# Turning the rows of queries and keys by an F32R product with an F32R identity instead of a transpose

## The reference

```python
q = (x @ wq.T); k = (x @ wk.T); v = (x @ wv.T)      # 16 heads of 8
diff_sq = q_norm_sq + k_norm_sq - 2.0 * qk
denom = maximum((1 - q_norm_sq) * (1 - k_norm_sq), 1e-6)
dist = arccosh(maximum(1 + 2 * diff_sq / denom, 1.0))
out = (softmax(-dist) @ v) @ wo.T
```

## Time and profile before

| | |
|---|---|
| Median of 3 runs | 2456.44 us (2451.4 to 2459.8) |
| Profiled execution, its own time | 2463.32 us |
| Its span | 2461.5 us |
| Mean granted clock of TensorE | 0.917 |
| Busy: PE, DVE, ACT, POOL | 2101.2, 1952.3, 1742.9, 1589.3 us |
| L1363 (turns of rows), MATMUL x1024 | 179.6 us busy |

### The profile page before, as it was taken

One profiled execution on the slowest core, in us unless ns is written; L12 is line 12 of the kernel. 1 busy time (PEld: TensorE's weight loads), 2 busy tenths in 40 slices (PEclk: granted clock), 3 DMA queues, 4 the chain that ended last, 5 costly groups with the idle time before them and its releaser, 6 DMA issues. The chain is left out here.

```text
span 2461.5 us, 50910 instructions
## 1 busy us (share of the span) xinstructions
PE 2101.2 (85%) x15592; PEld 1593.8 (65%) x15592; DVE 1952.3 (79%) x5939; ACT 1742.9 (71%) x3053; POOL 1589.3 (65%) x1609
## 2 busy tenths in 40 slices
PE   4999999999999997999996687778777878778776
PEld 4677777777777776888884455555555555555555
DVE  4677676777777775778776889999999999999982
ACT  2666666666666663444432799999999999999995
POOL 2767676666666740000002889999999898899992
PEclk7999999999999996999997569999999889998987
DMA  5000000000000003453440556666666666566663
GB/s 142 1 2 2 2 1 2 2 1 2 1 2 1 1 2 70 99 111 70 105 104 11 119 110 129 129 141 137 126 128 124 126 134 139 119 124 128 127 139 80
DMA packets 62954, 184.22 MB, mean 75 GB/s; under 512 B 7430, under 2 KB 29481, under 8 KB 46378
## 3 DMA queue, kind: packets, MB, share of 16 engines
q0 software_dynamic: 18432, 134.23, 27.1%
q1 hardware_dynamic: 36010, 43.38, 7.7%
q10 hardware_dynamic: 8320, 4.19, 0.7%
HBM read 42.85 MB, written 4.72 MB: 19 GB/s over the span
## 5 line engine op out<-in xcount | busy, mean ns | idle before, releaser
L1564 POOL TENSOR_TENSOR spare<-spare,u 128x1024 f32<-128x1024 f32 x224 | 530.8, 2370 | 18.7
L542 ACT ACTIVATE prob<-s_ps,nmax 128x128 f32<-128x128 f32 (+1 forms) x1024 | 364.4, 432 | 132.3 <-DVE nmax L599 132.3
L599 DVE CUSTOM_DVE_ANT_0 s_ps<-s_ps,mask 128x128 f32<-128x128 f32 (+1 forms) x1024 | 340.8, 386 | 100.5 <-issue 76.4
L579 POOL TENSOR_TENSOR g_lo<-g_all,g_hi 128x512 fp32r<-128x512 f32 x256 | 328.5, 1283 | 21.3
L1640 DVE TENSOR_SCALAR u<-d_ps 128x1024 f32<-128x1024 f32 x256 | 311.8, 1218 | 34.3 <-PE i_ps L1375 33.6
L1644 DVE SCALAR_TENSOR_TENSOR u<-i_ps,u 128x1024 f32<-128x1024 f32 x256 | 313.5, 1225 | 13.2 <-DVE u L1640 0.5
L1375 PE MATMUL d_ps<-rowsT 28*128 28x256 f32 x1024 | 137.1, 342 | 181.0 <-DVE u L1644 180.2
L1562 POOL TENSOR_SCALAR spare<-u 128x1024 f32<-128x1024 f32 x224 | 244.8, 1093 | 59.0 <-DVE u L1644 58.8
L534 ACT COPY g_all<-g_ps 128x512 f32<-128x512 f32 x256 | 151.5, 592 | 162.7 <-PE g_ps L63 161.5
L1521 ACT ACTIVATE u<-u 128x1024 f32<-128x1024 f32 x256 | 258.5, 1071 | 6.3 <-DMA u<-spare 6.1
L1375 PEld LDWEIGHTS d_ps<-rowsT 28*128 28x128 f32 x1024 | 87.4, 197 | 269.9 <-issue 265.6
(11 more groups left out here) (275 smaller groups left out, 5598.1 us busy)
## 6 DMA issues: line engine op xcount, KB each, us to landing
u<-spare POOLq DMA_DIRECT2D x128, 1024.0 KB, 9.6
w_all<-w_rows SPq DMA_DIRECT2D x128, 256.0 KB, 5.9
x<-L_attn_x ACTq DMA_DIRECT2D x8, 512.0 KB, 13.9
y<-x SPq DMA_DIRECT2D x32, 128.0 KB, 7.3
wkqv<-L_attn_Wkqv SPq DMA_DIRECT2D x4, 528.0 KB, 8.6
gate_rows<-L_ffn_gate_proj SPq DMA_DIRECT2D x1, 512.0 KB, 14.4
up_rows<-L_ffn_up_proj SPq DMA_DIRECT2D x1, 512.0 KB, 11.5
down_cols<-L_ffn_down_proj SPq DMA_DIRECT2D x1, 512.0 KB, 13.4
```

What stands on the lines that cost most here:

```text
L542: last = nc.scalar.activation(prob[:, kind, at, :].rearrange("p c n -> p (c n)"), s_ps[kind][:, at.start * P:at.stop * P], ACT.Exp, bias=n ...
L579: nc.gpsimd.tensor_tensor(g_lo[:, gb, q, :], g_all[:, h % 2, :], g_hi[:, gb, q, :], ALU.subtract).then_inc(g_split, 1)
L599: last = nc.vector.tensor_tensor_reduce(out=scores, in0=scores, in1=keep.mask[:, N - width:N], scale=-1.0, scalar=3.4e38, op0=ALU.add, op1 ...
L1564: nc.gpsimd.tensor_tensor(extra, extra, pair, ALU.mult).then_inc(prod_done, 1)
```

## The change

The four turns of a pair go from `nc.tensor.transpose`, which reads `rows` as plain float32 and an F32 identity, to an ordinary product in F32R: the rows are the stationary operand, an identity in F32R is the moving one. The identity's copy, `ident_r`, is made by VectorE in `rstd_of_all` (so twice), and takes 512 bytes of each partition. Products of 1.0 by numbers already rounded to F32R and sums with zeros leave the values as they are. All other turns stay transposes.

```diff
@@ rstd_of_all
                 nc.vector.memset(eps[:, :], LN_EPS).then_inc(eps_set, 1)
+                nc.vector.tensor_copy(keep.ident_r[:, :], keep.ident)
                 dve.wait_ge(std_done, 1)
@@ pe_turn_rows
-                    src = rows[:, side, j, 2 * p:2 * p + 2, :].rearrange("p h f -> p (h f)").bitcast(F32)
-                    last = nc.tensor.transpose(r_ps[p % 2][:, at:at + P], src, keep.ident)
+                    src = rows[:, side, j, 2 * p:2 * p + 2, :].rearrange("p h f -> p (h f)")
+                    last = nc.tensor.matmul(r_ps[p % 2][:, at:at + P], src, keep.ident_r[:, :], start=True, stop=True)
             last.then_inc(rows_turned, 1)
@@ Kept
         self.ident = self.ident_f[:, :]
+        self.ident_r = m.sb("ident_r", [P, P], F32R)
```

## The result

The changed kernel takes 2514.29 us in the median (2508.65 to 2517.41), the kernel before 2456.44 us in the same comparison. The ratio is 1.0239, 95% interval 1.0217 to 1.026: slower by 2.4%, 58 us. The forecast was slower by 24 us, 2480, with a range up to 2500. The direction is as forecast and the clock is the cause, but the loss is more than twice the size.

What follows compares the result with a forecast made beforehand. It took VectorE's work as the loop's floor, with half-clock time setting its waits for TensorE. Copy 0, turn pace 0 and clock falls +24 us on 2456.44 gave 2480 us; range 2443 to 2500, the forecast's own 2460 to 2500.

Steps and rivals of the forecast that it cites:

- What bounds the kernel: In the loop, VectorE's work is the floor, about 31 us a batch; time at half clock decides its waits for TensorE.
- The copy of the identity: VectorE's 128x128 copy, made twice, hides where VectorE waits for ScalarE's root; taken as 0, 0.6 us without cover.
- Time on the array: On TensorE, the longer weight load sets the F32R turn's pace at 0.11 us, as today, so no gain.
- Half the streaming: In the turns of rows TensorE streams 59 of 110 ns, so the clock falls in every batch and returns later.
- The sum: Each of the 27 steady batches goes from 33.43 to 34.32 us, +24.0 us; the first four add 0.
- The high bound: In the 27 steady batches, one more half-clock stretch than the 0.85 batch, at 0.76 us: +45 us, 2501.
- R1: On TensorE, longer loads occupy the array like streaming, so clock and time stay: 2456 us within 3; chance 0.18.
- R2: The F32R turn takes 0.22 us with the array full, the clock holds at 1.00: 2449 us; chance 0.16.
- R3: On TensorE, transposes don't count for the clock but products do, so it holds 1.00: 2437 us; chance 0.08.

Runs made afterwards that it cites:

- `ident_only`: The changed kernel with its transposes back, so only the copy of the identity and its place in memory are left: 2458.56 us, ratio 1.0012.
- `fill6_after`: The changed kernel with four unread F32 products at p = 6, ahead of the turn of attention: 2484.8 us, ratio 1.013 to the kernel before.
- `wide_rows`: The changed kernel with the identity twice side by side, so all but the last of four F32R products stream 256 columns: 2459.44 us, ratio 1.0018.
- `first_five`: The changed kernel with F32R products for the rows of pairs 0 to 4 only, transposes for 5 to 7: 2484.02 us, ratio 1.0133.
- `f32_product`: The kernel before with the turns of rows as ordinary F32 products, two instructions a turn: 2489.08 us, ratio 1.0146.
- `fill_before`: The kernel before with four unread F32 products at p = 7, ahead of the turn of x: 2481.92 us, ratio 1.0122.

## Why the prediction was right about the way and wrong about the size

*What bounds the kernel.* Right that the half clock sets how long VectorE waits for TensorE; but it is its place and not only its length that counts.

*The copy of the identity, 0.* Right: `ident_only`, 1.0012 with 1 in its interval.

*Time on the array, 0.11 us a turn, no gain.* Right, 0.12. VectorE waits 25.2 us for rows as before, and `fill6_after` has batches of 32.7 us. Twice the columns change the pace little (`wide_rows`), so the stream does not set it; that the load does is the nearest reading.

*Half the streaming, so the clock falls at the turn of every batch and comes back later.* Right, and shown by `wide_rows`: loads, format and pace kept, 7/8 of the streaming restored, and the loss is gone.

*The sum.* This is the step that failed: "A batch that stays at 0.50 for two stretches at that place is the one at 0.85: 34.32 us." That batch exists (34.59 us, at 0.85) but is only one of three. In the others the clock stays down for a third stretch, 35.5 and 35.6 us, since the eight turns of p = 0, which used to bring it back, stream half as well, and with them the whole MLP product of p = 0 runs at half clock. I had said this in words ("comes back later") and put no number to it. `first_five`, which keeps those eight as transposes, has the forecast's batch, 34.2, and 2484 us.

*The high bound, one stretch more for 0.76 us.* Too low for a bound, and the second half of the failed step: the price of a stretch was mis-sized. The third stretch costs 35.6 - 34.6 = 1.0 us, and 1.3 us against the 34.32 of my sum, because it lies over the rest of the MLP product of p = 0 and the pairs behind it (3.72 us for 1.95, VectorE's wait 2.56 for 1.18). With 35.6 and 35.5 in two of three batches and 34.6 in the third, 27 x (35.25 - 33.43) = 49 us. The 0.76 came from a batch whose stretch lies 10.5 us in, over the turns of p = 7. The earlier trace rows had the dearer place: its stretch at 2010.5 us stands in a batch of 34.10 us, 1.39 above 32.71. A bound with that price, 27 x (0.89 + 1.39) = 62 us, would have held the 58. And of those who wait for the turns I named ScalarE's copies but not `act_hi`, whose wait went from 31.5 to 78.0 us.

*R1* falls by the clock itself, 0.84 for 0.92, and by `wide_rows`. *R2* falls by the pace; its price for a turn of 0.22 us, 0.44 us a batch, was also about half of what `f32_product` shows. *R3*, and the rule of the Trainium skill that it rests on ("TensorE: Matmul & The Clock Gate", Part 4: PE-mode transpose), falls: transposes held the clock better than the ordinary F32R products that took their place, 0.92 against 0.84.

## What to carry to other kernels

A cheaper instruction on an engine that isn't the bound can slow the kernel, when what it did was keep the clock up: ask how long the array streams in the emptiest stretch, not only how fast it gets through. Where twice the columns don't change the pace, widening the moving operand keeps the clock up for nothing; here that was worth 55 us against the narrow turns, which brings back the kernel before and no more. Filler belongs ahead of the fall: at p = 6 the four products made the kernel 0.3% faster, one step later 1.2% slower, for there they stand behind the fall and use up the idle time that takes in its delay. And price a stretch at half clock by what stands under it, the MLP product of p = 0 or nothing that anybody waits for.

## What the runs showed that I had not expected

The batches repeat in a pattern. The kernel after repeats 34.6, 35.6, 35.5 us eight times over, `first_five` sits at 34.1 to 34.3 us for 23 batches running, and `fill_before` has six or so batches of 34.2 to 34.5, then one of 35.8 and two of 32.8 and 32.9, and again. My reading is that batches and falls keep step with each other, so that a small change in a batch moves the fall onto or off the path; that this is why `fill_before` fell in so many batches is argued from the pattern, and not shown by a run of its own.

A wider product over columns that the next one overwrites does no harm to the pace: eight wide turns take 1.15 us at full clock against 1.11 for the narrow ones.
